# Two chained attentions on one core: the algebra between them cut from two halves into four parts of 16 tiles

## What is computed

```python
def _L0_xattn_ref(tgt, memory, Wq, Wk, Wv):
    ...
    scores = jnp.einsum('bhqd,bhkd->bhqk', q, k) * scale
    probs = jax.nn.softmax(scores, axis=-1)
    att = jnp.einsum('bhqk,bhkd->bhqd', probs, v)
    att = att.transpose(0, 2, 1, 3).reshape(B, N, D)
    tgt2 = att[0]
    return tgt + tgt2

def _L1_xattn_ref(input_features, query_feature, ...):
    norm_X = _layernorm(input_features, norm1_w, norm1_b)
    norm_F_L = _layernorm(query_feature, norm2_w, norm2_b)
    attended = _attention(norm_F_L, norm_X, norm_X, scale)
    h = jax.nn.gelu(attended @ fc1_w.T + fc1_b, approximate=False)
    cross_attended = h @ fc2_w.T + fc2_b
    norm_cross = _layernorm(cross_attended, norm3_w, norm3_b)
    self_attended = _attention(norm_cross, norm_cross, norm_cross, scale)
    skip_connect = cross_attended + gamma1 * self_attended
    return norm_F_L + gamma2 * skip_connect
```

## Time and profile before

| | |
|---|---|
| median of 3 runs | 240.56 us (238.62 to 248.52) |
| profiled execution, device time | 240.99 us |
| its span, first to last instruction | 239.2 us |
| busy: PE / DVE / ACT / POOL | 213.3 (89%) / 188.0 (79%) / 151.0 (63%) / 139.9 us (58%) |
| transfers | 18.11 MB read, 8.39 MB written |

### The profile page before, as it was taken

How to read it: one execution, slowest core, us unless ns; L and a number is a source line. 1 busy time by engine, 2 the same in 40 slices (tenths; PEclk the granted TensorE clock), 3 DMA queues, 4 the chain that set the end, 5 groups by cost and what they waited for, 6 DMA issues and landing times.

```text
span 239.2 us, 4947 instructions
## 1 busy us (share of the span) xinstructions
PE 213.3 (89%) x1736; PEld 153.9 (64%) x1736; DVE 188.0 (79%) x363; ACT 151.0 (63%) x292; POOL 139.9 (58%) x212
## 2 busy tenths in 40 slices
PE   6999989697999999999999989999997499899750
PEld 6766656574977969779698786877684254455320
DVE  6888876999999988968799998971354655988773
ACT  2067774406678858678586995876587346777520
POOL 6000068576999999979959993900028888222330
PEclk9999999979999999999999999999999956999995
DMA  6990000055550454415455000000000004264458
GB/s 191 380 348 7 1 1 3 3 182 169 167 179 29 162 171 176 152 51 160 171 171 174 6 3 1 3 0 1 3 0 3 1 13 165 106 243 182 176 205 325
DMA packets 14712, 26.81 MB, mean 112 GB/s; under 512 B 1760, under 2 KB 1760, under 8 KB 14688
## 3 DMA queue, kind: packets, MB, share of 16 engines
q1 hardware_dynamic: 14688, 26.50, 32.3%
HBM read 18.11 MB, written 8.39 MB: 111 GB/s over the span
## 4 chain that ended last, share of the span: by engine, by line
PE 58%; DVE 24%; POOL 7%; issue 5%; ACT 5%; DVEq 0%; ACTq 0%; POOLq 0%
PE psum L1040 15%; PE psum L977 7%; DVE bn L372 6%; DVE xN L392 5%; PE psum L1048 5%; PE psum L932 3%; DVE Fall L586 3%; PE psum L1078 2%; PE psum L1155 2%; PE psum L990 2%; PE psum L1060 2%; PE psum L1188 2%; PE psum L947 2%; PE psum L1005 2%; PE psum L1018 2%
## 5 line engine op out<-in xcount | busy, mean ns | idle before, releaser
L1040 PE MATMUL psum<-XT,Fall 128*128 128x256 f32 x256 | 62.5, 389 | 1.7 <-ACT Fall L822 1.7
L1040 PEld LDWEIGHTS psum<-XT,Fall 128*128 128x128 f32 x256 | 47.3, 195 | 7.5 <-ACT Fall L822 2.2
L665 POOL TENSOR_SCALAR cN<-cN,nmean,rstd 128x256 f32<-128x256 f32 x64 | 38.2, 608 | 2.4 <-POOL rstd L652 2.3
L645 POOL TENSOR_TENSOR xN<-xN,tgt 128x512 f32<-128x512 f32 x28 | 35.7, 1277 | 1.6 <-DVE xN L392 1.6
L392 DVE TENSOR_SCALAR xN<-xN,bn,rstd 128x256 f32<-128x256 f32 x64 | 34.0, 575 | 0.7 <-POOL rstd L652 0.7
L845 ACT ACTIVATE PT<-psum 128x512 f32<-128x512 f32 x32 | 19.2, 599 | 24.3 <-PE psum L1048 24.2
L652 POOL TENSOR_TENSOR rstd<-vps,minus_half 128x8 f32<-128x8 f32 (+1 forms) x16 | 25.0, 1564 | 15.7 <-DVE vps L383 15.6
L852 ACT ACTIVATE E<-psum,nmax 128x256 f32<-128x256 f32 x64 | 26.8, 474 | 11.0 <-DVE nmax L531 10.9
L531 DVE TENSOR_REDUCE nmax<-psum 128x2 f32<-128x512 f32 x32 | 21.9, 685 | 13.9 <-PE psum L1040 13.4
L571 DVE TENSOR_REDUCE nm<-psum 128x4 bf16<-128x1024 f32 x16 | 19.5, 1221 | 12.0 <-PE psum L1123 12.0
L819 ACT ACTIVATE XT<-psum,b1s,w1s 128x512 f32<-128x512 f32 x32 | 23.1, 792 | 3.7 <-PE psum L977 3.7
(11 more groups left out here) (174 smaller groups left out, 361.0 us busy)
## 6 DMA issues: line engine op xcount, KB each, us to landing
cN<-ctx SPq DMA_DIRECT2D x32, 256.0 KB, 2.9
xN<-x SPq DMA_DIRECT2D x32, 256.0 KB, 4.0
out<-Fall SPq DMA_DIRECT2D x32, 256.0 KB, 2.3
x0T<-x0t SPq DMA_DIRECT2D x1, 256.0 KB, 2.7
wqT<-wqt SPq DMA_DIRECT2D x1, 256.0 KB, 3.2
c0T<-c0t SPq DMA_DIRECT2D x1, 256.0 KB, 3.8
wkT<-wkt SPq DMA_DIRECT2D x1, 256.0 KB, 5.6
wvT<-wvt SPq DMA_DIRECT2D x1, 256.0 KB, 5.8
```

The lines of the kernel that those rows point to most:

```text
L645: pool.tensor_tensor(xN[:, b % SLOTS, :], xN[:, b % SLOTS, :], tgt2[:, :, :].rearrange("p t d -> p (t d)"), ALU.add).then_inc(y_ok, 1)
L665: pool.tensor_scalar(own, own, nmean[:, p % 4, NT * m + t:NT * m + t + 1], root_of(p, 0, m, t), ALU.add, ALU.mult)\
L1040: last = pe.matmul(bank[SBANK1[b % 3]][:, t * N:(t + 1) * N], Fall[:, b, c, t * P:(t + 1) * P], XT[:, p % 4, c, m * N:(m + 1) * N], start= ...
```

## The change

It leaves the mathematics and moves the algebra. The 64 tiles go in four parts k of 16 tiles. Parts 0 to 2 share one Gelu over 48 tiles (24 batches, `SHARES[0]`), part 3 has its own. The keyed products are now taken of h, not of u, on GpSimd for all parts; DVE multiplies their sum by the root and adds K's last row (`left(k)`, two more instructions), since u is h times the root beside a constant 1.

```diff
+PART = TILES // 4
+SHARES = (slice(0, 3 * PART), slice(3 * PART, TILES))
+KEYED = (4, 8, 16, 24)
...
+        def scaled(k):
+            G = members(k)
+            for _ in range(NEWTON):
+                newton(var[:, G], r3[:, G], t3[:, G])
+            link(dve.tensor_tensor(u[:, G, 0:H + 1], ha[:, G, :], spread(r3[:, G], H + 1), ALU.mult), ("u", k))
+
+        def left(k):
+            G = members(k)
+            dve.wait_ge(summed_ok, KEYED[k])
+            if k >= 2:
+                dve.wait_ge(rooted_ok, 7 * (k - 1))
+            link(dve.tensor_tensor(uK[:, G, :], uK[:, G, :], spread(r3[:, G], U), ALU.mult))
+            link(dve.tensor_tensor(uK[:, G, :], uK[:, G, :],
+                                   K[:, U * (U - 1):U * U].unsqueeze(1).to_broadcast([P, PART, U]), ALU.add))
             left_cuts(uK[:, G, :], cut[:, G, 0:U], sU[:, 0, G, :], U)
...
-            for part in LATE.get(b, ()):
-                algebra(0, part)
+            if b == 27:
+                hidden_input(0)
+            if b == 29:
+                squares(0)
+                variance(0)
+            if b == 30:
+                scaled(0)
+            if b == 31:
+                left(0)
...
+        squares(1)
         maxima(0)
         saved(QUADS - 1)
+        variance(1)
+        scaled(1)
         for p in range(2 * QUADS + 5):
             if p + 1 < PAIRS:
                 maxima(p + 1)
...
+            if p == 0:
+                left(1)
+                hidden_input(1)
+            if p == 5:
+                left(2)
+            if p == 9:
+                left(3)
             if p >= 5:
                 finish(p - 5)
-            if p == 0:
-                algebra(1, 0)
-            if p == 4:
-                second_keyed(0)
-                second_left(0)
-            if p == 7:
-                second_left(1)
...
+        pool.wait_ge(zero_ok, 6)
+        pool.wait_ge(gelu_ok, 1)
+        keyed(0)
+        keyed(1)
         right(0)
-        weights5()
-        scaled(0)
+        squares(2)
         right(1)
+        keyed(2)
+        scaled(2)
         output_cuts(0)
-        scaled(1)
+        right(2)
+        pool.wait_ge(gelu_ok, 2)
+        squares(3)
         output_cuts(1)
-        keyed(1)
-        right(2)
-        for q in range(2, QUADS):
+        scaled(3)
+        output_cuts(2)
+        right(3)
+        keyed(3)
+        for q in range(3, QUADS):
             output_cuts(q)
...
             if k + 1 < PAIRS and (m == 1 or k + 1 >= EARLY):
                 evacuate(k + 1, m)
+            if b == 29:
+                hidden(0)
             if b >= 1:
                 weights_copied(b - 1)
...
-            if p == 1:
+            if p == 2:
                 hidden(1)
...
-            if p in (QUADS, QUADS + QUADS // 2):
-                h = (p - QUADS) // (QUADS // 2)
-                pe.wait_ge(alg, ALG["left", 1 + h])
-                pe.wait_ge(right_ok, 12 + 6 * h)
+            if p % 4 == 0:
+                pe.wait_ge(alg, ALG["left", p // 4])
+                pe.wait_ge(right_ok, 6 * (p // 4 + 1))
...
-            if b == 31:
-                scores(0)
             if b == B:
                 pe.wait_ge(V1_ok, QUADS)
                 keep_busy(4, 6)
             if b >= 1:
                 weights_turned(b - 1)
+            if b == B:
+                scores(0)
+                turn(1)
...
-            if b == 30:
+            if b == 31:
                 turn(0)
-            if b == 31:
-                turn(1)
         for p in range(2 * QUADS + 5):
-            if p < PAIRS:
-                maxima_turn(p)
             if p == 0:
                 keep_busy(3, 6)
                 apply(QUADS - 1)
+            if p < PAIRS:
+                maxima_turn(p)
```

More of the change, by code:

```diff
@@ L448, in newton @@
             link(dve.scalar_tensor_tensor(y, t, 1.5, y, ALU.add, ALU.mult))
[L450 to L462, removed]
-            left_cuts(uK[:, G, :], cut[:, G, 0:U], sU[:, 0, G, :], U)
[L464 to L484, removed]
-                link(dve.tensor_scalar(v, v, EPS, None, ALU.add))
-                link(dve.tensor_scalar(y.bitcast(I32), v.bitcast(I32), 1, None, ALU.logical_shift_right))
-                link(dve.tensor_scalar(y.bitcast(I32), y.bitcast(I32), -1.0, RSQRT_SEED, ALU.mult, ALU.add))
-                newton(v, y, t)
-            elif part == 4:
-                newton(v, y, t)
-                newton(v, y, t)
-                link(dve.tensor_tensor(u[:, G, 0:H + 1], ha[:, G, :], spread(y, H + 1), ALU.mult), ("u", g))
-            elif part == 5:
-                products(u[:, G, :], K[:, :], U)
-            elif part == 6:
-                link(dve.tensor_reduce(uK[:, G, :], produced(U), AX.X, ALU.add))
[L497 to L501, removed]
@@ new lines, in hidden_input @@
+        def hidden_input(g):
+            G = SHARES[g]
+            oa = OA[:, :, :, :, :].rearrange("p q t i k -> p (q t i) k")[:, G, :]
+            dve.wait_ge(o_saved, (6, QUADS)[g])
+            link(dve.reciprocal(rA[:, G].unsqueeze(2), oa[:, :, H:H + 1]))
+            link(dve.tensor_tensor(hpre[:, G, :], oa[:, :, 0:H], spread(rA[:, G], H), ALU.mult))
+            link(dve.tensor_tensor(hpre[:, G, :], hpre[:, G, :],
+                                   c_("fc1b").unsqueeze(1).to_broadcast([P, G.stop - G.start, H]), ALU.add), ("hpre", g))
@@ new lines, in squares @@
+        def squares(k):
+            G = members(k)
+            q = big[:, 0:PART * (H + 1) ** 2].rearrange("p (t j i) -> p t j i", t=PART, j=H + 1)
+            if k == 0:
+                dve.wait_ge(gelu_ok, 1)
+                dve.wait_ge(zero_ok, 6)
+            link(dve.tensor_tensor(q, ha[:, G, :].unsqueeze(2).to_broadcast([P, PART, H + 1, H + 1]),
+                                   Q[:, :].rearrange("p (j i) -> p j i", j=H + 1).unsqueeze(1)
+                                   .to_broadcast([P, PART, H + 1, H + 1]), ALU.mult))
+            link(dve.tensor_reduce(W5[:, G, :], q, AX.X, ALU.add))
@@ L826, in hidden @@
             act.wait_ge(alg, ALG["hpre", g])
-            act.activation(ha[:, members(g), 0:H], hpre[:, members(g), :], ACT.Gelu).then_inc(gelu_ok, 1)
+            act.activation(ha[:, SHARES[g], 0:H], hpre[:, SHARES[g], :], ACT.Gelu).then_inc(gelu_ok, 1)
         def turned_values(q):
@@ L874, in _ @@
                 applied(q - 1)
-            if b == 21:
-                hidden(0)
             if b == 29:
```

82 lines of the change are left out of this document (35 added, 47 removed).

## The result

The changed kernel is slower: 258.56 us (median of 4 runs, 256.04 to 258.74) against 239.75 (median of 4, 238.62 to 248.52) for the kernel before in the same session. The ratio is 1.075, with a 95% interval of 1.070 to 1.079. The profiled execution took 258.74 us. The forecast of 246.0 us and its range up to 250.5 are both missed; the sign was right.

What follows compares the result with a forecast made beforehand. PE bounds stage 1; in stage 2 its 3.24 us stop and slow clock cost 6.6. Full-clock terms +1.7 +3.0 +1.9 -3.3 -1.7 -0.6 +2.5 gave 244.5, plus 1.8 for the clock 246.3, forecast 246; range 239.5 to 250.5.

Steps and rivals of the forecast that it cites:

- the last one: Clock step: one of the new stops of 2.0, 2.95 and 3.1 us brings the clock down, adding 1.8 us.
- Rival E: Two clock falls, or one ahead of the 13 idle matmuls delaying p = 2: 251 us (249 to 253), chance 0.14.
- `left(0)` and `left(1)` at 1.9 us each: DVE's left cuts around the start of stage 2: 16-tile cuts 1.36 plus two new instructions of 0.27 each.
- Newton, +3.0: Start of stage 2: part 1's variance, Newton and u behind saved(7) delay maxima_turn(1), 3.0 us of it new.
- point (3): Expected sign: DVE spends 3.5 us between saved(7) and maxima(1), all on the chain of work that ended last.
- Second Gelu, +1.9: At p = 2, both table loads ahead of pair 2's exponential delay maxima_turn(3): +1.9 us.
- The stop before the first output turn, -3.3: Ahead of p = 5: PE's 3.24 us stop for GpSimd's first output cuts goes, taking the delay from +6.5 to +3.3.
- The slow stretch gone, -1.7 with `left(2)`: p = 5 and 6 at full clock take 5.8 plus 1.7 for left(2), so p = 7's delay falls to +1.6.
- `left(3)` waits for `keyed(3)`, +2.5: At p = 9, DVE stands 1.4 us for part 3's keyed products, then works 1.9; 2.5 us stay.
- point (6): Expected sign: DVE idle before left(3), released by GpSimd.
- Stage 1: Terms -1.7 + 1.5 + 1.7: algebra leaves the slots, PE stops in slot 29 for table loads, net delay at shift(0).
- point (1): Expected sign: PE's four-slot pace up to slot 28 is 14.85 us, with no wait for DVE.

Runs made afterwards that it cites:

- a1: Changed kernel with idle matmuls filling the three stops at the start of stage 2 (before turn(0), behind shift(0), behind attend(0)): 252.61 us, ratio 1.046.
- a2: a1 plus nine idle matmuls ahead of each of turn(8) and turn(12): 247.96 us, ratio 1.027.
- c4: a2 with 5 idle matmuls ahead of turn(0) and GpSimd's keyed(1) and squares(2) waiting until left(0) is done: 248.15 us.
- c2: a2 with part 1's variance and Newton work moved behind maxima(1), the idle matmuls moved with it: 247.71 us.
- c3: a2 with the second Gelu at p = 1 instead of p = 2, its input right behind saved(7), idle matmuls adjusted: 246.05 us, ratio 1.024.
- b1: Kernel before the change with 13 idle matmuls in its 3.24 us stop ahead of the first output turn: 239.78 us against 240.69, ratio 0.995.
- d1: a2 with both moves of c3 and c4 (second Gelu at p = 1, GpSimd's part 1 products after left(0)): 244.78 us, ratio 1.016.
- c5: d1 with left(2), left(3) a period earlier, keyed(3) ahead of output_cuts(1), no idle matmuls ahead of turn(8) and turn(12): 245.35 us, ratio 1.020.
- e1: d1 with only left(2) a period earlier, no idle matmuls ahead of turn(8), keyed(3) between output_cuts(2) and right(3): 245.22 us, ratio 1.025.
- a3: Changed kernel with left(2) and left(3) cut a period earlier and keyed(3) ahead of output_cuts(1): 249.94 us, ratio 1.036.
- c1: a1 with left(2) and left(3) cut a period earlier and keyed(3) ahead of output_cuts(1): 250.11 us, ratio 1.041.

## Why the prediction was wrong

**The step that failed is the last one**: "I expect that one of them brings the clock down, and take the smaller price, 1.8". Five stretches at 1.2 GHz came, and a1 and a2 price them at 10.6 us. These 8.8 us too little, and 3.5 in the sum at full clock, are the 12.3 us between 246.3 and the measured 258.56. Three errors are in that one sentence. The idle matmuls don't hold the clock when the stop lies ahead of them; they only run longer. The forecast's own stops of 1.7 and 2.5 us for `left(2)` and `left(3)` were counted as waits and never as stops that the clock could answer. And 1.8 was taken from a place where the clock was back after some eight matmuls (3.65 us). Rival E had the mechanism, but two falls of it, and 253 us at most.

The full-clock sum was 244.5, and a2 measures 248.0, 3.5 short, 3.0 of it by p = 3:

- *`left(0)` and `left(1)` at 1.9 us each*: 3.1 and 3.4, and Newton's first instruction 0.99 for 0.2. In c4 and c2 the same work takes 2.0. That is 1.1 us on the path at p = 0 (c4), most of the 1.5 that are missing at `shift(0)`. `left(1)` is about 1.4 longer ahead of `maxima(2)`, where PE waits 1.02 us for `nm` in a2; this is a difference of two rows, not tried alone, and in c2 the delay passed to the next instruction. The Trainium skill (SBUF — State Buffer, Who interferes with whom) says that a VectorE instruction with two inputs in SBUF, or one in a two-port mode, and a GpSimd instruction that reads SBUF exclude each other, and that the second to start stands still until the first ends. The trace agrees: 164.12 against 164.09. It spoke against a change that puts two parts on each of these engines at the same time, and I left it out.
- *Newton, +3.0*: the work takes 3.3 us (178.67 to 181.96) for 3.6, from `shift(0)` to p = 1 the delay grows from 3.1 to 6.2 us, and point (3) holds. But that it stands between `saved(7)` and `maxima(1)` is not what costs; moved away, it gives nothing (c2).
- *Second Gelu, +1.9*: 2.3 (c3). Right, and so is point (4): p = 3 begins 5.36 us after p = 2, released by `wqT`.
- *The stop before the first output turn, -3.3*: right. From p = 3 to 6 a2 needs 7.8 us and b1 11.1; there is no wait for `sC` in the changed kernel (point 5).
- *The slow stretch gone, -1.7 with `left(2)`*: right at full clock, as a2 needs 7.74 us from p = 5 to 7 where the kernel before needs 9.24. In the changed kernel itself the clock fell again, and they take 8.40. What is wrong is the view that the kernel before loses 3.4 us by that stretch: without it, it gains 1.1 (b1), since GpSimd's next output cuts hold PE instead.
- *`left(3)` waits for `keyed(3)`, +2.5*: right at full clock, the amount (a2 has 8.74 us from p = 10 to 12, b1 5.76) and the reason. VectorE stands still for GpSimd in a2, 0.98 us for the forecast's 1.4:

```profile
214.81 0.26 DVE L480 TENSOR_TENSOR uK<-uK,r 128x96 f32<-128x96 f32 x1 [0.98 <-POOL uK L709]
```

  It does so in d1 too, 1.00 us. In the changed kernel point (6) fails, as the slow stretches have made stage 2 so late that `keyed(3)` is done (222.12) when VectorE reaches `left(3)` (223.50); there PE waits 1.42 us for the cut itself and 0.60 for the `finish` behind it.
- *Stage 1*: point (1) holds. The four-slot steps are 14.84, 14.85 and 14.85 us up to slot 28. The stop for `vT` is 1.28 for 1.5, that before `turn(0)` 3.48 for 2.0 (point 2).

Point (7), a slow stretch at the start and none at p = 5 and 6, fails in its second half: the clock falls again at 210 us, in p = 6. That the sign was right owes little to the step that failed: at full clock a2 is 2.7 per cent above the kernel before.

## What to carry to other kernels

Price a stop of TensorE by its length plus the clock behind it, and count the short stops too as ones that may bring it down; run the kernel once with idle matmuls in the stops, which separates both parts in a single run (here 10.6 of 18.8 us). Work that is split over two engines to run side by side is worth the sum of its rows only if neither holds the other up: look in the trace for the same instruction with two durations. And before you take a wait away, see what the engine behind it is short of. In b1, c5 and e1 the wait that went was followed by one for the next entry in GpSimd's list.

## What the hardware showed beyond that

- Stops of 1.40 and 0.60 us, shortly after one another, were followed by half clock (0.54 and 0.50 from 210 to 220 us), and in e1 so were 1.10 and 0.28 us. In a2, with idle matmuls in the first gap and the second of 0.6 us left, the clock stayed at 1.00.
- Not every short stop does this. In d1 the clock stays at 1.00 behind stops of 1.28 us (for `vT`) and 1.10 us (`turn(0)`), and in b1 behind those of 1.19 and 1.24. What decides is not shown by these runs.
- A slow stretch ends after very different times: that behind 183 us ended with the idle matmuls at 190, that behind 210 lasted to 220 us, and in a3 one lasted from 197 to 213 us with no idle time in PE's rows between.
- Which of VectorE and GpSimd is held depends on who starts first: where VectorE's 128x400 product starts 0.12 us ahead (a2, at 160.46 us), it takes its 0.57 us and GpSimd's product 1.48 instead of 1.17.
- Behind the last matmuls VectorE still forms results and they are stored (in a2 VectorE is busy and the transfers move 372 GB/s from 240 to 242.5 us). The span ends 14.9 to 16.5 us after p = 15 begins in all profiles but c1's first; what makes this difference of 1.6 us was not tried.
